# A mixture-of-experts feed-forward's scratch rows renumbered by chunk, its results stored two tiles at a time

## Chip, cores and metric

One core of one Trainium2 chip runs the whole program. The metric is the device time in microseconds, lower is better. The engines are TensorE (PE, its weight loads PEld), VectorE (DVE), ScalarE (ACT), GpSimd (POOL) and SyncE (SP), which here only issues transfers.

## The reference, cut to what matters

Two layers act on x, [4, 512, 256] float32, that is 16 tiles of 128 tokens. Layer 0 is cross attention and a small mixture of experts; layer 1 is cross attention with 16 heads and then this feed-forward, which the change touches:

```
def _L1_ffn_ref(x, router_w, router_b, w1, b1, w2, b2, sw1, sb1, sw2, sb2):   # E = 64, K = 8, H = 64
    xf = x.reshape(-1, d_)
    probs = jax.nn.softmax(xf @ router_w + router_b, axis=-1)
    tw, ti = jax.lax.top_k(probs, K)
    tw = tw / jnp.sum(tw, axis=-1, keepdims=True)
    ...  # routed: sum over the 64 experts of cw[:, None] * (silu(xf @ W1 + B1) @ W2 + B2)
    return (routed + shared).reshape(b_, s_, d_)   # shared: two dense experts of width 512
x = x + _L1_ffn_ref(_layernorm(x, axis=-1), ...)
```

## The kernel before, in words

Everything is written out by hand: each engine has one program (`d_sync`, `d_pe`, `d_act`, `d_dve`, `d_pool` for the last feed-forward), and semaphores join them. `wait_from(engine, semaphore, value)` is such a wait.

**The routed experts.** The 64 experts form 32 pairs of 64 + 64 hidden columns. The tokens are taken in two halves g = 0, 1 of 8 tiles. Each of the 8 x 1024 (token, expert) choices of a half gets a position: positions are grouped by pair and each pair starts on a multiple of 128, so the half has NX = 95 tiles of 128 rows, of 256 floats (1 KB) each. `x_starts`, `x_positions` and `x_places` work the positions out on DVE: `x_rk` holds the position of each token at each expert, `dve.max` (L2185) takes the eight of a token, and L2187 converts them to integers, `x_at`. POOL reads `x_at` in `x_scatter` (L2289), which writes the normalised token rows into the HBM scratch `zs2[g]` by 64 indirect transfers of 128 rows, and later in `x_gather` (L2325), which reads the result rows from `ys2[g]` by 64 more. `x_sum` (L2336) adds them, weighted, to X on DVE. `zs2` is first filled with zeros (`x_fill`, L1976). Layer 0's small expert stage works in the same way on scratch of its own, and loads its chunks into `e_z`.

**The loop over tiles.** The 2 x 95 = 190 tiles (GXN) run through one loop of all engines. A chunk is four tiles of a half (the last has three), 24 chunks a half. SP loads a chunk with one transfer (`load_chunk`, L2404) into one of three buffers `xt_z`: a partition gets four rows of 1 KB which lie 128 rows apart in HBM. PE transposes tile q + 3 (L2461), ACT copies it to `xt_zt` (L2553, four buffers) and copies the pair's weights to `xt_w1c` (L2569), PE multiplies tile q + 2 (L2471), ACT applies silu (L2579), DVE masks (L2650), PE multiplies tile q by the second weights (L2492), and DVE copies the result from PSUM to `xt_y` (L2658, four buffers of one tile). SP stores each tile by a transfer of its own, 128 rows of 1 KB (L2416).

**The order on SP's queue** is written out: in `d_sync`, L2411 to L2416, for every tile q: if q begins chunk c, first issue the load of chunk c + 2; then wait for `y_out` of tile q and issue its store. So the load of chunk c + 2 is issued behind the store of the last tile of chunk c - 1. The load of the second half's first chunk also waits for the second scatter (L2401).

**Where the plan is made.** The first half's planning runs on DVE between pieces of attention (`routing` in `w_dve`, x_places at unit 24), the second half's inside the loop (`tick` of `d_dve`: ranks at q = 2, places at q = 3, owners at q = 10, tables at q = 14). DVE does the ticks in order between its masks and copies, and from q = 110 on eight sums (L2343) in every ten ticks. Behind the loop, `d_dve` splits the second shared expert's weights and runs the shared experts of u = 2 to 7 (`d_hidden`, `second`); the second half's gather and sums run beside them, and the program ends with the last 32 sums and the store of X.

Of the kernel before, what the change touches and what calls it, by code (L numbers as in the profile page):

```python
# [5 lines left out]
F32 = mybir.dt.float32  # L6
# [9 lines left out]
P = 128  # L16
# [23 lines left out]
NYX = 4  # L40
# [36 lines left out]
def build_program(nc, x, ctxT, ctx, mask, cols, rows, l0_wqT, l0_wkT, l0_wv, l0_w1, l0_w2, gate_wT,  # L77
                  mlp1, mlp2, mlp1_bT, mlp2_b, l1_wp, router_w, l1_w1, l1_w2, l1_b2,
                  x1_w1, x1_w2, x1_b1, out):
    with ExitStack() as ctx_all:  # L80
# [56 lines left out]
        zs2 = [nc.dram_tensor(f"zs2{g}", [NX * P, D], F32).ap() for g in range(2)]  # L137
        ys2 = [nc.dram_tensor(f"ys2{g}", [NX * P, D], F32).ap() for g in range(2)]
# [148 lines left out]
        xt_y = [sb(f"xt_y{i}", [P, D]) for i in range(NYX)]  # L287
# [3 lines left out]
        xt_zt = [sb(f"xt_zt{i}", [P, KD, P]) for i in range(4)]  # L291
# [4 lines left out]
        xt_s = [sb(f"xt_s{i}", [P, P]) for i in range(3)]  # L296
        x_k.append([sb(f"x_k{j}1", [P, XT_N, TOP1])[:, :, :] for j in range(3)])
# [1656 lines left out]
        PL_N, OWN_N = 11, 11  # L1954
# [21 lines left out]
        def x_fill(sp, g, part):  # L1976

            if g == 0 and part == 0:
                wait_from(sp, XR["zero"], 1)
            n0, n1 = part * 12, min(part * 12 + 12, NX)  # L1980
            sp.dma_start(zs2[g][n0 * P:n1 * P].rearrange("(n p) d -> p n d", p=P),
                         x_zero[:, :].unsqueeze(1).to_broadcast([P, n1 - n0, D])).then_inc(XR[f"fill{g}"][0], 16)
        FILLS = -(-NX // 12)
# [197 lines left out]
        def x_places(dve, g):  # L2181

            wait_from(dve, XR["pos"], 2 * g + 2)
            for i in range(XT_N):
                dve.max(x_top[g][:, i, :], x_rk[:, i, :]).then_inc(XR["top"][0], 1)  # L2185
            wait_from(dve, XR["top"], (g + 1) * XT_N)
            dve.tensor_copy(x_at[g], x_top[g]).then_inc(XR["at"][0], 1)  # L2187
# [121 lines left out]
        def x_stored(eng, q):  # L2309
            for i in range(NYX):  # L2310
                wait_from(eng, XT[f"stored{i}"], 16 * len(range(i, q, NYX)))

# [12 lines left out]
        def x_gather(pool, g):  # L2325
            x_stored(pool, (g + 1) * NX)
# [49 lines left out]

        def chunk_at(q):
            g, n = q // NX, q % NX
            return g * NXC + n // 4, n % 4
# [6 lines left out]
        def d_sync(sp):  # L2386
# [8 lines left out]
            def load_chunk(c):  # L2395
                g, qs = c // NXC, chunk_tiles(c)
                if c % NXC == 0:
                    x_all_scattered(sp, g)
                if c < 3:
                    sp.wait_ge(DM["y"], 1)  # L2400
                else:  # L2401
                    wait_from(sp, XT["t"], chunk_tiles(c - 3)[-1] + 1)
                n0 = qs[0] % NX
                sp.dma_start(xt_z[c % 3][:, 0:len(qs), :],  # L2404
                             zs2[g][n0 * P:(n0 + len(qs)) * P].rearrange("(n p) d -> p n d", p=P)).then_inc(XT[f"zin{c % 3}"][0], 16)
# [5 lines left out]
            for q in range(GXN):  # L2411
# [3 lines left out]
                wait_from(sp, XT["y_out"], q + 1)  # L2415
                sp.dma_start(ys2[q // NX][q % NX * P:(q % NX + 1) * P], xt_y[q % NYX][:, :]).then_inc(XT[f"stored{q % NYX}"][0], 16)  # L2416
# [3 lines left out]
        def d_pe(pe):  # L2420
# [43 lines left out]
            def first(q):  # L2464
# [5 lines left out]
                for k in range(KD):  # L2470
                    last = pe.matmul(PS[:, 2 + q % 2, 0:P], xt_w1c[q % 3][:, k, :], xt_zt[q % 4][:, k, :], start=k == 0,  # L2471
                                     stop=k == KD - 1)
# [65 lines left out]
        def d_act(act):  # L2538
# [10 lines left out]
            def turned(q):  # L2549
# [3 lines left out]
                act.activation(xt_zt[q % 4][:, :, :], PS[:, q % 2, 0:D].rearrange("p (k t) -> p k t", k=KD), ACT.Copy  # L2553
# [66 lines left out]
        def d_dve(dve):  # L2620
# [32 lines left out]
            def out_of(q):  # L2653
# [59 lines left out]
            split(1)  # L2713
            for u in range(FIRST, DU):
# [1182 lines left out]
```

## Time and profile before

| | |
|---|---|
| median of 3 runs | 1397.46 us (1397.35 to 1398.76) |
| the profiled execution's own time | 1403.52 us |
| its span in the trace | 1401.3 us |
| mean granted TensorE clock | 0.974 |
| busy: PE / PEld / DVE / ACT / POOL | 92% / 71% / 70% / 63% / 31% |
| the loop over the 190 tiles | about 1033 to 1302 us |
| transfers: `ys<-xt_y` / `xt_z<-zs` | 190 of 128 KB / 46 of 512 KB and 2 of 384 KB |

Times are microseconds from the span's start. An engine's idle time is put down to what released it. In a row of the timeline, the bracket at the end holds the idle time before the work and its releaser. SPq rows are the issues of transfers on SP's queue; the transfer itself lasts beyond its issue. The DMA share is the mean busy share of the core's 16 DMA engines.

### The profile page before, as it was taken

The page shows a single profiled execution, that of the slowest core. Times are in us where ns is not written, and L with a number is a line of the kernel's source. Part 1 is how long each engine was busy: PE and PEld are TensorE (multiplying, and loading weights), DVE is VectorE, ACT ScalarE, POOL GpSimd, SP SyncE. Part 2 cuts the span into 40 slices and gives each one's busy share as a digit, 9 for nine tenths or more (in the row PEclk, how much of TensorE's full clock was granted, in tenths as well). Part 3 has the DMA queues.
Part 4 walks back from the last instruction along what each step waited for, and adds up shares of the span by engine and source line. Part 5 has one row for each costly group of instructions (what it writes and reads, how often), then busy time and mean ns, then how long its engine had stood idle before and what let it go on. Part 6 is the DMA issues. An engine that isn't in the chain of part 4 may idle for free.

```text
span 1401.3 us, 28443 instructions
## 1 busy us (share of the span) xinstructions
PE 1290.4 (92%) x9262; PEld 997.0 (71%) x9262; DVE 983.5 (70%) x2775; ACT 879.2 (63%) x2147; POOL 436.3 (31%) x457
## 2 busy tenths in 40 slices
PE   7999998997999979999999999999978999988993
PEld 6899897885556656667676666666676777777893
DVE  7767764465656768887788887988547655777665
ACT  5556664334766656777787785778436777777540
POOL 0000001234055160610001000677206763454574
PEclk9999999999999999999999999999989999999997
DMA  9522200413365230332632400232356887888343
GB/s 349 201 77 74 76 24 17 164 76 121 132 194 192 75 95 3 111 102 99 202 126 87 159 17 9 76 122 84 133 201 225 298 290 231 255 268 259 102 133 98
DMA packets 147627, 194.65 MB, mean 139 GB/s; under 512 B 14639, under 2 KB 129941, under 8 KB 146453
## 3 DMA queue, kind: packets, MB, share of 16 engines
q1 hardware_dynamic: 132117, 150.79, 32.3%
q0 software_dynamic: 15360, 41.96, 9.3%
q8 instruction: 81, 1.33, 0.4%
q14 instruction: 69, 0.57, 0.1%
HBM read 107.77 MB, written 84.93 MB: 138 GB/s over the span
## 4 chain that ended last, share of the span: by engine, by line
PE 66%; DVE 14%; DMA 7%; ACT 5%; issue 5%; POOL 1%; ACTq 1%; SPq 0%; DVEq 0%; POOLq 0%
PE PS L72 9%; PE PS L73 8%; PE PS L74 8%; PE PS L3292 7%; DMA xt_z<-zs 6%; PE PS L1416 6%; PE PS L3264 5%; PE PS L2471 3%; PE PS L3279 3%; PE PS L2492 3%; PE PS L3307 3%; PE PS L1432 2%; DVE a_pt L971 2%; PE PS L1310 2%; PE PS L2461 2%
## 5 line engine op out<-in xcount | busy, mean ns | idle before, releaser
L3414 ACT ACTIVATE c_pt<-PS 100x512 f32<-100x512 f32 x256 | 138.8, 595 | 92.3 <-PE PS L3279 91.7
L3405 ACT ACTIVATE c_pr<-c_sm,c_mn 128x400 f32<-128x400 f32 x256 | 158.8, 626 | 18.1 <-DVE c_mn L3554 18.1
L3554 DVE CUSTOM_DVE_ANT_0 c_sm<-PS,c_mw 128x400 f32<-128x400 f32 x256 | 136.0, 568 | 11.1 <-PE PS L3264 9.7
L2471 PE MATMUL PS<-xt_zt,xt_w1c 128*128 128x128 f32 x760 | 124.0, 287 | 9.2 <-ACT xt_w1c L2569 5.5
L3292 PE MATMUL PS<-c_pt,c_v 100*64 100x512 f32 x512 | 125.8, 613 | 0.0
L3264 PEld LDWEIGHTS PS<-c_k,c_q 64*128 64x128 f32 x768 | 63.0, 189 | 82.9 <-issue 49.8
L2492 PE MATMUL PS<-xt_w,xt_h 128*128 x380 | 116.2, 388 | 3.7 <-DVE xt_y L2658 3.6
L2471 PEld LDWEIGHTS PS<-xt_zt,xt_w1c 128*128 128x128 f32 x760 | 102.7, 197 | 20.8 <-ACT xt_w1c L2569 19.2
L3264 PE MATMUL PS<-c_k,c_q 64*128 64x400 f32 x768 | 106.3, 382 | 9.2 <-DVE c_mn L3554 8.6
L449 POOL TENSOR_TENSOR rs<-ve,halfneg 128x4 f32<-128x4 f32 x12 | 13.8, 1147 | 321.0 <-DVE ve L464 228.3
L3563 DVE TENSOR_SCALAR c_pr<-c_pr,c_rl 128x400 f32<-128x400 f32 x256 | 106.8, 459 | 4.5
L2553 ACT ACTIVATE xt_zt<-PS 128x256 f32<-128x256 f32 x190 | 72.2, 381 | 57.1 <-PE PS L2461 56.4
L1416 PE MATMUL PS<-e_w,e_zt 128*128 x184 | 90.9, 618 | 3.3 <-issue 1.6
L2461 PE MATMUL PS<-ident,xt_z 128*128 128x128 f32 x380 | 75.6, 282 | 16.8 <-DMA xt_z<-zs 12.8
L2658 DVE COPY xt_y<-PS 128x256 f32<-128x256 f32 x190 | 79.7, 419 | 15.8 <-DMA ys<-xt_y 14.2
L2569 ACT ACTIVATE xt_w1c<-xt_w 128x256 f32 x190 | 78.1, 412 | 18.8 <-issue 18.6
L2332 POOL DMA_INDIRECT xt_rows<-ys,R x64 | 62.5, 977 | 75.3 <-DVE X L2343 30.0
L2461 PEld LDWEIGHTS PS<-ident,xt_z 128*128 128x128 f32 x380 | 51.7, 143 | 43.7 <-DMA xt_z<-zs 23.7
L3279 PEld LDWEIGHTS PS<-ident,c_pr 64*100 64x100 f32 x2048 | 76.7, 126 | 8.5 <-issue 0.8
L3279 PE MATMUL PS<-ident,c_pr 64*100 64x64 f32 x2048 | 79.3, 218 | 0.0
L2332 POOL DMA_INDIRECT xt_rows<-ys,x_keep x64 | 63.9, 998 | 36.8 <-issue 18.9
L2300 POOL DMA_INDIRECT zs<-x_stage,R x64 | 64.9, 1014 | 19.3 <-issue 17.1
(407 smaller groups left out, 3488.2 us busy)
## 6 DMA issues: line engine op xcount, KB each, us to landing
ys<-xt_y SPq DMA_DIRECT2D x190, 128.0 KB
xt_z<-zs SPq DMA_DIRECT2D x46, 512.0 KB
zs<-x_zero SPq DMA_DIRECT2D x14, 1536.0 KB, 6.9
xt_w<-x_w SPq DMA_DIRECT2D x4, 2048.0 KB, 15.3
a_cT<-ctxT SPq DMA_DIRECT2D x4, 1601.0 KB
a_raw_nat<-ctx SPq DMA_DIRECT2D x4, 1536.0 KB
zs<-e_zero SPq DMA_DIRECT2D x2, 2944.0 KB, 19.4
ys<-e_y SPq DMA_DIRECT2D x46, 128.0 KB
```

The costliest lines, as they stand in the source:

```text
L72: pe.matmul(out, w[0], x[0], start=first, stop=False)
L1416: last = pe.matmul(PS[:, 2 + q % 2, :], e_zt[q % 3][:, k, :], w[:, 0, k, :], start=False, stop=k == KD - 1, skip_group_check=True)
L2332: pool.indirect_dma_start(x_rows(n)[:, k, :], None, ys2[g][:, :], bass.IndirectOffsetOnAxis(ap=x_at[g][:, i, k:k + 1], axis=0)).then_inc(x ...
L2461: last = pe.transpose(PS[:, q % 2, k * P:(k + 1) * P], xt_z[c % 3][:, n, k * P:(k + 1) * P], ident[:, :])
L2471: last = pe.matmul(PS[:, 2 + q % 2, 0:P], xt_w1c[q % 3][:, k, :], xt_zt[q % 4][:, k, :], start=k == 0, stop=k == KD - 1)
L2492: pe.matmul(PS[:, 4 + q % 2, 0:D], xt_h[q % 3][:, :], xt_w2[:, bass.ds(pair[q], 1), :].squeeze(1), start=True, stop=True).then_inc(XT["y"] ...
L3264: last = pe.matmul(PS[:, BS + h, 0:WIN], c_q[u % 2][a][hs, i * P:(i + 1) * P], c_k[u % 2][c][hs, :], start=n == 0, stop=n == 2)
L3279: last = pe.transpose(PS[0:KW, BT + r, (h * 4 + t) * DH:(h * 4 + t + 1) * DH], c_pr[s % 3][h][half, t * KW:(t + 1) * KW], ident[half, half])
L3292: last = pe.matmul(PS[h * DH:(h + 1) * DH, BU, :], c_v[ph % 2][0:KW, t, p * P + h * DH:p * P + (h + 1) * DH], c_pt[u % 2][0:KW, h, t, :], ...
L3405: act.activation(c_pr[s % 3][h][:, :], c_sm[h][:, :], ACT.Exp, bias=c_mn[:, s % 4, h:h + 1], scale=-1.0, accum_out=c_l[:, s % 4, h:h + 1]) ...
L3414: act.activation(c_pt[u % 2][0:KW, :, :, i * P + r * DH:i * P + (r + 1) * DH].rearrange("p h t q -> p (h t) q"), PS[0:KW, BT + r, :].rearr ...
L3554: dve.tensor_tensor_reduce(c_sm[h][:, :], PS[:, BS + h, 0:WIN], c_mw[:, b * QT + i, :], 1.0, BIG, ALU.add, ALU.min, c_mn[:, s % 4, h:h + 1 ...
```

## The change

Rows of `zs2` and `ys2` are renumbered. Before, row p of tile n of a half was row 128 n + p. After, in chunk c = n // 4, it is row 512 c + 4 p + n % 4, so that the four rows of a partition lie together. `x_places` works the new number out of the old one by nine more operations of DVE on [128, 64] floats, in seven steps that wait for each other, ahead of the conversion; it borrows three slices of `x_rk` as scratch. A load of a chunk then takes 4 KB per partition from one place. The result tiles are stored by two: `xt_y` has three buffers of two tiles, and SP issues one transfer of 2 KB per partition when the second tile is done (48 a half; the last of a half carries one tile). `xt_y` moves in SBUF to beside `xt_z`, where it overlaps `d_h`, so DVE waits for all stores (`x_stored(dve, 1)`) before the shared experts; `xt_zt` has three buffers for four. The scratch tensors grow from 95 to 96 tiles, and the fill with them.

```diff
-        zs2 = [nc.dram_tensor(f"zs2{g}", [NX * P, D], F32).ap() for g in range(2)]
+        zs2 = [nc.dram_tensor(f"zs2{g}", [4 * NXC * P, D], F32).ap() for g in range(2)]
...
-        xt_y = [sb(f"xt_y{i}", [P, D]) for i in range(NYX)]
...
-        xt_zt = [sb(f"xt_zt{i}", [P, KD, P]) for i in range(4)]
+        xt_zt = [sb(f"xt_zt{i}", [P, KD, P]) for i in range(2)]
+        xt_y = [sb(f"xt_y{i}", [P, 2, D]) for i in range(NYX)]
...
+        xt_zt.append(sb("xt_zt2", [P, KD, P]))
...
             for i in range(XT_N):
                 dve.max(x_top[g][:, i, :], x_rk[:, i, :]).then_inc(XR["top"][0], 1)
-            wait_from(dve, XR["top"], (g + 1) * XT_N)
-            dve.tensor_copy(x_at[g], x_top[g]).then_inc(XR["at"][0], 1)
+            top = g * TOP_N + XT_N
+            tile, chunk, at = (x_rk[:, h, :].rearrange("p (i k) -> p i k", k=TOP1) for h in range(3))
+            wait_from(dve, XR["top"], top)
+            dve.tensor_scalar(tile, x_top[g], 0.5 - P / 2, 1.0 / P, ALU.add, ALU.mult).then_inc(XR["top"][0], 1)
+            dve.tensor_scalar(at, x_top[g], 4.0, None, ALU.mult).then_inc(XR["top"][0], 1)
+            wait_from(dve, XR["top"], top + 2)
+            dve.tensor_scalar(chunk, tile, 1.5 * BIG23, None, ALU.add).then_inc(XR["top"][0], 1)
+            wait_from(dve, XR["top"], top + 3)
+            dve.tensor_scalar(tile, chunk, 1.5 * BIG23, None, ALU.subtract).then_inc(XR["top"][0], 1)
+            wait_from(dve, XR["top"], top + 4)
+            dve.tensor_scalar(chunk, tile, -1.5, 0.25, ALU.add, ALU.mult).then_inc(XR["top"][0], 1)
+            dve.scalar_tensor_tensor(at, tile, 1.0 - 4 * P, at, ALU.mult, ALU.add).then_inc(XR["top"][0], 1)
...
+            dve.scalar_tensor_tensor(tile, chunk, 4.0 * (P - 1), at, ALU.mult, ALU.add).then_inc(XR["top"][0], 1)
+            wait_from(dve, XR["top"], top + 9)
+            dve.tensor_copy(x_at[g], tile).then_inc(XR["at"][0], 1)
...
+        def in_chunk(rows, c):
+            at = c % NXC * 4 * P
+            return rows[c // NXC][at:at + 4 * P].rearrange("(p n) d -> p n d", n=4)
+
+        def two_at(q):
+
+            n = q % NX
+            return q // NX * NX2 + n // 2, n % 2, n % 2 == 1 or n == NX - 1
...
-                n0 = qs[0] % NX
-                sp.dma_start(xt_z[c % 3][:, 0:len(qs), :],
-                             zs2[g][n0 * P:(n0 + len(qs)) * P].rearrange("(n p) d -> p n d", p=P)).then_inc(XT[f"zin{c % 3}"][0], 16)
+                sp.dma_start(xt_z[c % 3][:, 0:len(qs), :], in_chunk(zs2, c)[:, 0:len(qs), :]).then_inc(XT[f"zin{c % 3}"][0], 16)
...
-                wait_from(sp, XT["y_out"], q + 1)
-                sp.dma_start(ys2[q // NX][q % NX * P:(q % NX + 1) * P], xt_y[q % NYX][:, :]).then_inc(XT[f"stored{q % NYX}"][0], 16)
+                j, m, last = two_at(q)
+                if last:
+                    wait_from(sp, XT["y_out"], q + 1)
+                    sp.dma_start(in_chunk(ys2, c)[:, n - m:n - m + 2, :], xt_y[j % NYX][:, :, :]
+                                 ).then_inc(XT[f"stored{j % NYX}"][0], 16)
...
-                wait_from(dve, XT[f"stored{q % NYX}"], 16 * (q // NYX))
-                dve.tensor_copy(xt_y[q % NYX][:, :], PS[:, 4 + q % 2, 0:D]).then_inc(XT["y_out"][0], 1)
+                j, m, last = two_at(q)
+                if m == 0:
+                    wait_from(dve, XT[f"stored{j % NYX}"], 16 * (j // NYX))
+                dve.tensor_copy(xt_y[j % NYX][:, m, :], PS[:, 4 + q % 2, 0:D]).then_inc(XT["y_out"][0], 1)
...
             split(1)
+            x_stored(dve, 1)
```

## Rows read from the trace of the kernel before

**Rows 1.** The page: the span; the chain that ended last by line.

```profile
span 1401.3 us, 28443 instructions
...
PE PS L72 9%; PE PS L73 8%; PE PS L74 8%; PE PS L3292 7%; DMA xt_z<-zs 6%; PE PS L1416 6%; PE PS L3264 5%; PE PS L2471 3%; PE PS L3279 3%; PE PS L2492 3%; PE PS L3307 3%; PE PS L1432 2%; DVE a_pt L971 2%; PE PS L1310 2%; PE PS L2461 2%
```


**Rows 2.** Window, L2461 alone: PE, PEld (counts), clock, DMA share, GB/s.

```profile
1084.20:1285.80 201.60, 59.51 (x302) 40.60 (x302) 0.99 0.85 268
```


**Rows 3.** Timeline: first matmuls of two chunks that waited for no load.

```profile
1244.24 0.71 PE L2471 MATMUL PS<-xt_zt,xt_w1c 128*128 128x128 f32 x4
...
1249.01 0.71 PE L2471 MATMUL PS<-xt_zt,xt_w1c 128*128 128x128 f32 x4
```


**Rows 4.** Chain of waits in order of time (start us, us, what): two loads.

```profile
1180.48 6.70 DMA xt_z<-zs
...
1236.18 6.37 DMA xt_z<-zs
```


**Rows 5.** Waits, 1040 to 1304 us: us in total, times, longest.

```profile
PEld PS L2461 <- DMA xt_z<-zs: 23.7, 30, 2.5
...
DVE xt_y L2658 <- DMA ys<-xt_y: 14.2, 18, 2.0
```


**Rows 6.** Timeline: a load's issue, and the transpose that needed it.

```profile
1252.47 0.47 SPq L2404 DMA_DIRECT2D xt_z<-zs  x1
...
1257.49 0.44 PE L2461 MATMUL PS<-ident,xt_z 128*128 128x128 f32 x2 [0.33 <-DMA xt_z<-zs]
```


**Rows 7.** Tile xt_z: issues of its loads (ns min/median/max).

```profile
L2404 SPq DMA_DIRECT2D xt_z<-zs x48: 371/434/2008, 1018.3 to 1291.4; - x48
```


**Rows 8.** Windows: PE, PEld, DVE, ACT, POOL busy; PEclk, DMA share, GB/s.

```profile
1016.00:1020.00 4.00, 2.99 (x27) 2.68 (x25) 1.57 (x4) 1.34 (x2) 0.00 (x0) 1.00 0.99 426
1123.00:1143.00 20.00, 18.51 (x125) 15.10 (x124) 10.59 (x30) 14.67 (x47) 16.00 (x16) 1.00 0.89 297
1163.00:1183.00 20.00, 18.83 (x127) 15.37 (x126) 10.79 (x33) 15.05 (x47) 4.28 (x5) 1.00 0.69 212
1187.00:1192.00 5.00, 4.78 (x23) 4.14 (x24) 1.89 (x5) 2.71 (x8) 3.78 (x5) 0.66 1.02 363
```


**Rows 9.** The tile x_stage: POOL's second scatter, first and last start.

```profile
L2300 POOL DMA_INDIRECT zs<-x_stage,x_keep x64: 957/971/1117, 1058.1 to 1148.6; - x64
```


**Rows 10.** DMA issues by line: KB each, median us from issue to landing.

```profile
e_z<-zs SPq DMA_DIRECT2D x9, 512.0 KB, 4.3
...
out<-X SPq DMA_DIRECT2D x4, 512.0 KB, 3.4
```


**Rows 11.** Timeline of DVE: small dependent operations; the conversion.

```profile
870.64 0.18 DVE L2157 TENSOR_SCALAR x_cq<-x_cp 128x32 f32<-128x32 f32 x1
870.86 0.18 DVE L2159 TENSOR_SCALAR x_cp<-x_cq 128x32 f32<-128x32 f32 x1
...
881.64 0.20 DVE L2187 CAST R<-R 128x64 int32<-128x64 f32 x1
```


**Rows 12.** Timeline of PEld: the next scores wait for DVE.

```profile
884.82 0.48 PEld L3264 LDWEIGHTS PS<-c_k,c_q 64*128 64x128 f32 x6 [0.81 <-DVE c_mn L3554]
```


**Rows 13.** Timeline: the second half's conversion, then PE.

```profile
1056.27 0.20 DVE L2187 CAST x_keep<-x_keep 128x64 int32<-128x64 f32 x1
...
1057.39 0.69 PE L2492 MATMUL PS<-xt_w,xt_h 128*128 x2 [1.91 <-DVE xt_y L2658]
```


**Rows 14.** Timeline of POOL: the first issue of each gather.

```profile
1177.50 1.02 POOL L2332 DMA_INDIRECT xt_rows<-ys,R  x1 [27.93 <-DMA ys<-xt_y]
...
1305.03 1.90 POOL L2332 DMA_INDIRECT xt_rows<-ys,x_keep  x1 [17.57 <-DMA ys<-xt_y]
```


**Rows 15.** Timeline behind the loop: DVE's split, last sums, last gather.

```profile
1304.88 1.23 DVE L2642 TENSOR_TENSOR d_w<-d_w1r,d_w 128x1024 fp32r<-128x1024 f32 x1
...
1384.58 13.27 DVE L2343 SCALAR_TENSOR_TENSOR X<-xt_rows,x_keep,X 128x256 f32<-128x256 f32 x25
...
1386.93 1.14 POOL L2332 DMA_INDIRECT xt_rows<-ys,x_keep  x1 [0.30 <-issue]
```

More of the change, by code:

```diff
@@ L39 @@
 NXC = -(-NX // 4)
-NYX = 4
+NX2 = -(-NX // 2)
+NYX = 3
 HEADS, DH = 16, 64
@@ L136, in build_program @@
         ys = [nc.dram_tensor(f"ys{g}", [NB * P, D], F32).ap() for g in range(GR)]
-        zs2 = [nc.dram_tensor(f"zs2{g}", [NX * P, D], F32).ap() for g in range(2)]
-        ys2 = [nc.dram_tensor(f"ys2{g}", [NX * P, D], F32).ap() for g in range(2)]
+        zs2 = [nc.dram_tensor(f"zs2{g}", [4 * NXC * P, D], F32).ap() for g in range(2)]
+        ys2 = [nc.dram_tensor(f"ys2{g}", [4 * NXC * P, D], F32).ap() for g in range(2)]
         def col(name, j):
@@ L1953, in build_program @@
         PIECES = 7
-        PL_N, OWN_N = 11, 11
+        PL_N, OWN_N, TOP_N = 11, 11, XT_N + 9
         FIELD = (NP - 1).bit_length()
@@ L1979, in x_fill @@
                 wait_from(sp, XR["zero"], 1)
-            n0, n1 = part * 12, min(part * 12 + 12, NX)
+            n0, n1 = part * 12, min(part * 12 + 12, 4 * NXC)
             sp.dma_start(zs2[g][n0 * P:n1 * P].rearrange("(n p) d -> p n d", p=P),
                          x_zero[:, :].unsqueeze(1).to_broadcast([P, n1 - n0, D])).then_inc(XR[f"fill{g}"][0], 16)
-        FILLS = -(-NX // 12)
+        FILLS = -(-4 * NXC // 12)
         def x_router_sync(sp):
@@ L2185, in x_places @@
                 dve.max(x_top[g][:, i, :], x_rk[:, i, :]).then_inc(XR["top"][0], 1)
-            wait_from(dve, XR["top"], (g + 1) * XT_N)
-            dve.tensor_copy(x_at[g], x_top[g]).then_inc(XR["at"][0], 1)
+            top = g * TOP_N + XT_N
[10 more added lines that the diff above has]
+            dve.scalar_tensor_tensor(at, tile, 1.0 - 4 * P, at, ALU.mult, ALU.add).then_inc(XR["top"][0], 1)
+            wait_from(dve, XR["top"], top + 6)
+            dve.tensor_scalar(tile, chunk, 1.5 * BIG23, None, ALU.add).then_inc(XR["top"][0], 1)
+            wait_from(dve, XR["top"], top + 7)
+            dve.tensor_scalar(chunk, tile, 1.5 * BIG23, None, ALU.subtract).then_inc(XR["top"][0], 1)
+            wait_from(dve, XR["top"], top + 8)
+            dve.scalar_tensor_tensor(tile, chunk, 4.0 * (P - 1), at, ALU.mult, ALU.add).then_inc(XR["top"][0], 1)
+            wait_from(dve, XR["top"], top + 9)
+            dve.tensor_copy(x_at[g], tile).then_inc(XR["at"][0], 1)
         def x_owners(dve, g):
@@ L2307, in x_all_scattered, with x_stored @@
                 wait_from(eng, XR[f"scat{g}{i}"], XT_N // 2 * TOP1 * 16)
-        def x_stored(eng, q):
+        def x_stored(eng, g):
             for i in range(NYX):
-                wait_from(eng, XT[f"stored{i}"], 16 * len(range(i, q, NYX)))
+                wait_from(eng, XT[f"stored{i}"], 16 * len(range(i, (g + 1) * NX2, NYX)))
         def x_rows(n):
@@ L2325, in x_gather @@
         def x_gather(pool, g):
-            x_stored(pool, (g + 1) * NX)
+            x_stored(pool, g)
             for i in range(XT_N):
@@ L2470, in first @@
                 for k in range(KD):
-                    last = pe.matmul(PS[:, 2 + q % 2, 0:P], xt_w1c[q % 3][:, k, :], xt_zt[q % 4][:, k, :], start=k == 0,
+                    last = pe.matmul(PS[:, 2 + q % 2, 0:P], xt_w1c[q % 3][:, k, :], xt_zt[q % 3][:, k, :], start=k == 0,
                                      stop=k == KD - 1)
@@ L2552, in turned @@
                     act.wait_ge(DM["y"], 1)
-                act.activation(xt_zt[q % 4][:, :, :], PS[:, q % 2, 0:D].rearrange("p (k t) -> p k t", k=KD), ACT.Copy
+                act.activation(xt_zt[q % 3][:, :, :], PS[:, q % 2, 0:D].rearrange("p (k t) -> p k t", k=KD), ACT.Copy
                                ).then_inc(XT["zt"][0], 1)
```

## The prediction

> **What bounds the kernel now.** I read the page first: its chain is mostly matmuls, but one transfer stands among them, `xt_z<-zs`, with 6% of a span of 1401.3 us, about 80 us in a stage that has only 190 tiles [rows 1]. That share overstates what can be won, since PE works during most of a load. So I measured the loop against itself. The window over the transposes counts 302 matmuls of L2461 in 201.6 us, two a tile, so 151 tiles at 1.335 us [rows 2]. Where no load is late, the first matmuls of two neighbouring chunks lie 1249.01 - 1244.24 = 4.77 us apart, 1.193 us a tile [rows 3]. 151 tiles at that pace are 180.1 us, so 21.5 us of the stretch are lost. The chain of waits in order of time shows where: it passes through 14 loads, up to 6.37 and 6.70 us from issue to the transpose [rows 4]. The waits of the loop agree in size: PEld waited 30 times, 23.7 us, for a load; DVE waited 18 times, 14.2 us, for a store that still held its `xt_y` [rows 5].
>
> Why are the loads late? One is issued at 1252.47, and the transpose that needs it starts at 1257.49 after an idle time of 0.33: at the unstalled pace a load has some 4.7 us from issue to need [rows 6]. The issue of a load has a median of 434 ns but a longest of 2008 ns: SP's queue is then held up itself [rows 7]. And the DMA engines are near full: with POOL's scatter running, their share is 0.89 at 297 GB/s, against 0.69 at 212 where POOL is mostly idle [rows 8]. POOL's 64 scatters start over 90.5 us, one of 128 KB each 1.44 us [rows 9]; the loop at its unstalled pace wants 2 x 128 KB each 1.193 us beside them, together 311 GB/s, a share of 0.93 on the mean of the engines. So loads come late by what queues up.
>
> **The change, part by part.**
>
> *Cheaper packets.* From the same windows, time per KB on one of 16 engines is share x 16 x 1024 / rate: 0.89 gives 49 ns where nearly everything is 1 KB rows, 0.99 and 426 GB/s give 38 ns where the weight tables come in rows of 16 KB [rows 8]. No row shows 4 KB or 2 KB packets alone, so these two are the bounds: a gain of nothing, and of 11 ns per KB. I take a fixed part per packet plus a part per KB that fits both, 11.7 + 37.3 ns: 40.2 ns per KB for a load in 4 KB packets, 43.1 for a store in 2 KB packets. A tile needs 8 KB of each per engine and 6.6 KB of POOL's. Before that is 22.6 x 49 = 1107 ns of 1193, 93%; after it is 8 x 40.2 + 8 x 43.1 + 6.6 x 49 = 990 ns, 83%. What the engines move at the share of 0.89 rises from 297 to about 332 GB/s against 311 wanted, so the backlog should mostly go, though not all: the lead of 4.7 us stays as written, a load of 512 KB in 1 KB rows took 4.3 us even in the lightly loaded first expert stage (`e_z`), and a store of that size 3.4 [rows 10]. Its own transfer becomes 0.28 us shorter, but a store of two tiles stands in front of it instead of one, 0.3 us longer. The gain is in the queue, not in the single load.
>
> Of the 21.5 us, some 1.7 belong to the clock: behind the load of 6.70 us that landed at 1187.2 the mean granted clock was 0.66 for 5 us, a part of it at 1.2 instead of 2.4 GHz, and 5 x 0.34 = 1.7 [rows 4, 8]. The other 19.8 are load waits. Bounds: none or all of them go. I take three quarters, 14.9 us, since the computed capacity is above what is wanted but the lead is no longer, and 1 us of the clock's.
>
> The Trainium skill speaks against it ("DMA: Bandwidth & Descriptors", section "Why small descriptors are slow (HBM only)"): the cost is about 3 cycles per packet beside one per 32 bytes, and merging pays only at 256 bytes or less. By that, 1 KB costs 35 cycles and 4 KB 131, only 6% less per KB where my fit has 18%; the sum would then end near the second rival's below.
>
> *Stores by two.* 96 issues for 190, each of 0.3 us; SP mostly waits, so I count nothing. The buffers hold six tiles instead of four, and a pair is waited for five tiles behind its issue instead of nearly four: DVE's 14.2 us should nearly vanish, but they lie inside the same stalls and are not counted again.
>
> *The new row numbers.* Nine operations in seven dependent steps on DVE, twice. Small dependent operations start 0.22 us apart, and one on 128x64 lasts 0.20 against 0.18 [rows 11]. Seven steps at 0.24, two of them with a second operation at 0.1, make 1.9 us. In the first half they stand behind L2187 at 881.64, and from there to the next scores DVE is busy throughout: PE's weight load at 884.82 had waited 0.81 for DVE [rows 12]. So they are on the path: +1.9. In the second half they stand behind 1056.27, and at 1057.39 PE had waited 1.91 for DVE: again on the path, +1.9 [rows 13]. Bounds for each: nothing if later slack takes it back, 2.5 with a lower clock behind the longer wait. POOL's scatters start 1.9 us later: the second runs from 1058.1 to 1148.6, would end near 1151, and its first reader, load 24, is issued near q = 88. With the loop at full pace that is about 1159, so the wait for it stays covered by some 6 us; if that cover went, SP's queue would stand, stores included [rows 9].
>
> *The gathers* wait for the stores of their half, at 1177.50 and 1305.03. They move with the loop [rows 14]. A last store of 256 KB lands perhaps 0.4 us later, and the last gather, issued at 1386.93, serves the last 8 of the 25 sums that begin at 1384.58 and take 0.53 each, so at 1393.6, over 6 us behind its issue: covered. The new wait of DVE for all stores stands behind its split, which starts at 1304.88, about when the gather found them stored: covered too, and queued behind it is only `low` of u = 2, which waits for ACT anyway [rows 15].
>
> *Three buffers `xt_zt` for four:* PE transposes tile q + 3 only after it has multiplied tile q + 1, so no new wait. The larger fill, 256 KB more, lies in attention: nothing.
>
> **Sum.** 1.9 + 1.9 - 14.9 - 1.0 = -12.1 us. The profiled execution took 1403.52 (span 1401.3 and 2.2 around it), which becomes 1391.4; it lies 6.1 above the median of the runs, and against the median of 1397.46 the forecast is 1385.4. Its own range, with 60% to 90% of the load waits gone and 2 to 5 us of DVE, is 1381 to 1390.
>
> **Rivals.**
>
> *All of it goes.* No load is late: -19.8 - 1.7 + 3.8 = -17.7, so 1379.8, and down to 1377 if DVE's work is partly covered. For it: the capacity estimate, and the queue's held issue of 2 us. Against it: the lone 4.3 us of `e_z` are near the lead of 4.7 with nothing queued. Chance 0.15.
>
> *The packets are not cheaper.* The 38 ns may be due to the tables' stage having reads only, without stores beside them. Then 1 KB costs the same in any packet, demand stays at 93%, and only fewer issues and the deeper store buffers help: a third of the waits, -6.6 + 3.8 = -2.8, so 1394.7. Chance 0.17. The rule of the Trainium skill cited above points to this rival.
>
> *Slower: the doubled store in front of each load.* SP's queue issues a 256 KB store immediately before every load (L2404 behind L2416). If the packets are no faster, each load lands 8 x 49 = 0.39 us later. Paid at the 14 to 30 loads that are waited for, that is 5 to 12 us; with DVE's 3.8 it makes 1406 to 1413, taken as 1408. It decides if a load's own gain stays under 0.39 us and the backlog does not shrink. Against it: SP's queue carries the same bytes in a quarter of the packets. Chance 0.10.
>
> *The change does not do what it says:* the transfers are still cut into 1 KB packets, and only DVE's 3.8 us stay, 1401.3. Against it: both sides are contiguous for 4 KB and 2 KB. Chance 0.03. The forecast keeps 0.55.
>
> **How the numbers follow.** A difference under 0.2%, 2.8 us, can't be told from none. Faster: 0.55 + 0.15 and half of the second rival, 0.78; within 0.2%: its other half, 0.09; slower: the last two, 0.13. Leaving out the slow cases and half of the lowest, the range is 1377 to 1395.
>
> **What would show it.** The DMA packets should fall by some 18,200 (46 x 384 + 2 x 256) for the loads and 12,000 (94 x 128) for the stores, the DMA share in the loop to 0.8 with the rate up to 300 GB/s, and L2461's waits for a load from 23.7 to about 6 us. The 151 tiles should take some 186 us. L2187 should come 1.9 us after the last maximum in both halves. The forecast is wrong if loads still take 5 us or more while POOL runs, if load 24 waits for the scatter, or if the clock falls again behind PE's longer wait near 1058.

## The result, and the profile after

The changed kernel took 1405.27 us in the median of 20 runs (1400.04 to 1414.82), the kernel before, run beside it, 1400.03 (1395.11 to 1407.60). The ratio is 1.0035 with a 95% interval of 1.0018 to 1.0052: 5 us slower, where 12 us faster were forecast. Single runs of one kernel spread over 12 to 15 us, more than the effect; the two profiled executions have spans of 1401.3 and 1400.9 us, so their spans say nothing, and their rows must be read for what waits for what.

The page of the changed kernel, its span and its DMA packets:

```profile
span 1400.9 us, 28274 instructions
...
DMA packets 116169, 195.15 MB, mean 139 GB/s; under 512 B 13135, under 2 KB 80053, under 8 KB 114997
```

The packets fell from 147,627 to 116,169, by 31,458 where some 30,200 were forecast. So the transfers are cut as the change says. Yet the waits that this was to remove stand where they were. The loads in its chain of waits, in order of time (19 are in that chain now, 14 before) [rows 4]; PEld's wait for a load, in the waits of 1040 to 1304 us [rows 5]; and the issues of the loads, with the time from issue to landing below (min/median/max, us) [rows 7]:

```profile
1180.83 5.76 DMA xt_z<-zs
...
1240.64 6.42 DMA xt_z<-zs
```

```profile
PEld PS L2491 <- DMA xt_z<-zs: 23.6, 26, 2.2
```

```profile
L2432 SPq DMA_DIRECT2D xt_z<-zs x48: 320/432/1565, 1018.0 to 1289.6; - x48
...
DMA to landing us min/median/max: 3.5/5.1/10.1
```

23.6 us in 26 waits, where it was 23.7 in 30. A load of 4 KB rows lands after 5.1 us in the median (the trace records the landing of 16 of the 48 loads), and the lead, the time from a load's issue to the transpose that needs it, is still about 4.7.

The landing is not the same everywhere. Here are the landings and PEld's waits for a load in three stretches: beside POOL's second scatter (1058 to 1148 us), with POOL nearly idle (1150 to 1177), and beside its gathers (1180 to 1295):

```profile
DMA to landing us min/median/max: 4.5/5.0/5.3
PEld PS L2491 <- DMA xt_z<-zs: 6.1, 9, 0.9
...
DMA to landing us min/median/max: 3.7/3.9/4.2
PEld PS L2491 <- DMA xt_z<-zs: 1.5, 2, 0.8
...
DMA to landing us min/median/max: 4.8/5.6/5.8
PEld PS L2491 <- DMA xt_z<-zs: 16.0, 15, 2.2
```

So with POOL nearly idle a load lands well within its lead, beside the scatter it takes a little more than the lead, and beside the gathers, where two thirds of the waits lie, 0.9 us more. (The two waits of the middle stretch include that for a load issued at 1147.07, still beside the scatter.) DVE's 14.2 us of waiting for a store are gone; no such row is left. The window over the transposes [rows 2] holds 306 matmuls, 153 tiles, in the time in which there were 151:

```profile
1084.20:1285.80 201.60, 59.50 (x306) 40.92 (x305) 1.00 0.82 271
```

That is 2.6 us for the loop's steady part, in one execution of each kernel. The windows [rows 8], with PE, PEld, DVE, ACT, POOL busy, the granted clock, the DMA share and GB/s:

```profile
1123.00:1143.00 20.00, 18.58 (x127) 15.84 (x128) 11.21 (x32) 15.23 (x48) 16.01 (x16) 1.00 0.82 292
1163.00:1183.00 20.00, 19.24 (x131) 16.14 (x130) 11.03 (x33) 16.04 (x50) 3.45 (x4) 1.00 0.69 220
1187.00:1192.00 5.00, 4.51 (x31) 3.57 (x29) 2.31 (x7) 3.86 (x12) 3.78 (x5) 1.00 0.92 292
```

With the scatter running, the share fell from 0.89 to 0.82 at nearly the same rate (292 GB/s for 297), so packets did become cheaper there (46 ns per KB for 49); with POOL nearly idle it is 0.69 at 220 GB/s for 212. The engines have more room and the loop does not use it.

The nine new operations, from the timeline: the last maxima, the first and the conversion, and then PE behind its wait for DVE [rows 13]. In the first half, PEld behind DVE [rows 12]:

```profile
1053.80 1.12 DVE L2187 MAX8 x_keep<-x_rk 128x8 f32<-128x64 f32 x8
...
1054.95 0.20 DVE L2191 TENSOR_SCALAR x_rk<-x_keep 128x64 f32<-128x64 f32 x1
...
1056.82 0.20 DVE L2207 CAST x_keep<-x_rk 128x64 int32<-128x64 f32 x1
...
1057.97 1.21 PE L2522 MATMUL PS<-xt_w,xt_h 128*128 x2 [2.38 <-DVE xt_y L2690]
```

```profile
885.01 0.48 PEld L3297 LDWEIGHTS PS<-c_k,c_q 64*128 64x128 f32 x6 [2.10 <-DVE c_mn L3587]
```

They run from 1054.95 to 1056.82, 1.87 us, and PE's wait is 2.38 us where it was 1.91. In attention, PEld waits 2.10 us where it waited 0.81. So the waits for a load that the change was to remove are still there, and what it added stands on the path. Behind the loop, DVE's split and the gather's first issue lie as before [rows 14, 15]:

```profile
1304.41 1.23 DVE L2672 TENSOR_TENSOR d_w<-d_w1r,d_w 128x1024 fp32r<-128x1024 f32 x1
...
1305.05 1.42 POOL L2352 DMA_INDIRECT xt_rows<-ys,x_keep  x1 [19.45 <-DMA ys<-xt_y]
```

### The profile page after: what moved, and what is told of

It reads as the page before. It is cut to its first block, busy times and chain, and to the rows that moved or that the text cites. A ratio compares the mean times of both kernels' runs of the same rounds, so it can differ in the third digit from the quotient of the medians.

```text
span 1400.9 us, 28274 instructions
## 1 busy us (share of the span) xinstructions
PE 1287.7 (92%) x9262; PEld 993.0 (71%) x9262; DVE 986.2 (70%) x2793; ACT 879.9 (63%) x2147; POOL 438.5 (31%) x457
## 2 busy tenths in 40 slices
DMA packets 116169, 195.15 MB, mean 139 GB/s; under 512 B 13135, under 2 KB 80053, under 8 KB 114997
## 4 chain that ended last, share of the span: by engine, by line
PE 64%; DVE 15%; DMA 8%; ACT 5%; issue 5%; POOL 1%; ACTq 1%; SPq 0%; DVEq 0%; POOLq 0%
PE PS L73 9%; PE PS L74 8%; PE PS L75 8%; DMA xt_z<-zs 7%; PE PS L3325 6%; PE PS L1418 6%; PE PS L3297 5%; PE PS L3312 3%; PE PS L2501 3%; PE PS L3340 3%; PE PS L1434 2%; PE PS L2522 2%; DVE a_pt L973 2%; PE PS L1312 2%; DVE c_sm L3587 2%
## 5 line engine op out<-in xcount | busy, mean ns | idle before, releaser
L2599 ACT ACTIVATE xt_w1c<-xt_w 128x256 f32 x190 | 78.1, 412 | 18.5 <-issue 18.3
L2491 PEld LDWEIGHTS PS<-ident,xt_z 128*128 128x128 f32 x380 | 52.3, 144 | 44.3 <-DMA xt_z<-zs 23.6
## 6 DMA issues: line engine op xcount, KB each, us to landing
xt_w<-x_w SPq DMA_DIRECT2D x4, 2048.0 KB, 14.9
```

What stands on the lines that cost most here:

```text
L2491: last = pe.transpose(PS[:, q % 2, k * P:(k + 1) * P], xt_z[c % 3][:, n, k * P:(k + 1) * P], ident[:, :])
```

## The experiments

Two theories stood against each other. **L**: a load is late because its own time from issue to landing is longer than its lead on SP's queue. **Q**: it is late because the DMA engines lack capacity and a backlog builds up. Each ratio is against the kernel before, timed beside it, with its 95% interval.

### The plan operations alone, and the change without them

```diff
 # e1, on the kernel before: the new operations, their result not used
+            top = g * TOP_N + XT_N
+            tile, chunk, at = (x_rk[:, h, :].rearrange("p (i k) -> p i k", k=TOP1) for h in range(3))
...
+            wait_from(dve, XR["top"], top + 9)
             dve.tensor_copy(x_at[g], x_top[g]).then_inc(XR["at"][0], 1)
```

> Edit: the kernel before, with the nine new operations of DVE in x_places, whose result is not used (old row numbers, old loads and stores). Theory L (a load is late by its own time from issue to landing, against a lead of some 4.7 us, and not by a backlog of the DMA engines; the change then leaves the load waits as they are and costs only DVE's planning): +2 to +4 us over before, 1.001 to 1.003, most of the change's loss; the second half's conversion comes 1.87 us later and the rest of the loop is as before. Rival S (the loss comes from the stores by two that stand in front of the loads): about +1 us or none, since there is neither a longer store nor another load here.

```diff
 # e2, on the changed kernel: the nine operations out, everything else in
-            dve.tensor_scalar(tile, x_top[g], 0.5 - P / 2, 1.0 / P, ALU.add, ALU.mult).then_inc(XR["top"][0], 1)
...
-            dve.tensor_copy(x_at[g], tile).then_inc(XR["at"][0], 1)
+            dve.tensor_copy(x_at[g], x_top[g]).then_inc(XR["at"][0], 1)
```

> Edit: the changed kernel with the nine operations left out, so that rows are scattered and gathered by the old numbers while loads and stores use the new layout (tiles then hold rows of other pairs; the amount and order of work is the same). Theory L: within 2 us of before (0.999 to 1.001), with load waits of PEld in the loop still 20 to 25 us. Rival S: still +3 us or more. A third theory, Q (packets did ease the DMA engines and DVE's planning ate the gain): 3 us or more faster than before, with load waits under 18 us.

e1 took 1406.64 us against 1399.92, ratio 1.0039 (1.0023 to 1.0056). e2 took 1398.23, ratio 0.9978 (0.9957 to 0.9998). The operations alone cost 5.5 us (0.0039 of 1399.9; 3.2 to 7.8), as much as the whole change loses and more than the 2 to 4 expected; the layout and the stores by two gain 3 us (0.3 to 6.0). That is between what L and Q expected of e2 (under 2, over 3), but its waits are not under 18 us, as Q has it. They stand at 27.6, in an execution that was the longest of the twelve (1407.87 us). And e1, whose loads have 1 KB rows, shows what the page of before did not, how long those take to land:

```profile
PEld PS L2473 <- DMA xt_z<-zs: 27.6, 27, 3.1
```

```profile
L2422 SPq DMA_DIRECT2D xt_z<-zs x48: 370/435/1976, 1018.6 to 1290.7; - x48
...
DMA to landing us min/median/max: 3.8/5.1/11.7
```

5.1 us in the median (of 32 recorded loads), the same as 4 KB rows. In the three stretches above the medians of e1 are 4.7, 4.2 and 5.6 us, those of the changed kernel 5.0, 3.9 and 5.6. So where loads are late, beside POOL's transfers, larger packets do not make them land sooner. With POOL nearly idle they may by 0.3 us, which is what the prediction computed for the load's own transfer, but that rests on four and two loads.

e1's windows show where the operations cost. Here are, in order, the kernel before from 860 to 900 us, and e1 there and from 1050 to 1070 us:

```profile
860.00:900.00 40.00, 37.15 (x310) 25.28 (x306) 33.82 (x124) 23.71 (x61) 14.38 (x14) 0.91 0.13 44
```

```profile
860.00:900.00 40.00, 35.62 (x302) 24.70 (x298) 33.61 (x127) 22.10 (x56) 12.92 (x13) 0.91 0.10 35
1050.00:1070.00 20.00, 15.14 (x86) 12.97 (x86) 14.35 (x60) 9.80 (x30) 8.96 (x9) 0.83 0.47 150
```

In attention PE is busy 1.5 us less of the same 40 (35.62 for 37.15). In the loop the mean granted clock from 1050 to 1070 is 0.83, where the kernel before has 0.91; the changed kernel has 0.81 there. PE waits longer for DVE and more of the following stretch is at 1.2 instead of 2.4 GHz, by 20 x 0.08 = 1.6 us. It was so in all four profiles that have the nine operations in one block in the loop (the changed kernel, e1 and, below, e3 and e9: 0.81 to 0.83), and in none of the ten that have none there (0.91 to 1.00). With the operations in three pieces (e10 and e14 below) it is 0.79 and 1.00. This stretch alone does not show a net price: over 1000 to 1300 us the mean granted clock is 0.97 in the kernel before, in the changed kernel and in e1 alike.

The clocks of whole executions do. Their mean is 0.9769 over the 78 runs of the kernel before that were timed beside the experiments, and 0.9745 over the 20 runs of the changed kernel, 0.9747 over 12 of e1 and 0.9750 over 6 of e3; without the nine operations it is 0.9765 (e2) and 0.9770 (e7). Among the runs of the kernel before, the 17 at 0.975 took 1403.3 us on average and the 11 at 0.980 took 1398.2, about 1 us for each 0.001. By that, e1's 0.0022 (give or take 0.0015) are worth some 2 us of its 5.5, an estimate.

### The loads issued earlier

```diff
 # e3 on the changed kernel, e4 on the kernel before
-                if n == 0 and c >= 1 and c + 2 < 2 * NXC:
-                    load_chunk(c + 2)
+                if n == 1 and c + 3 < 2 * NXC:
+                    load_chunk(c + 3)
```

> Edit: the changed kernel with each load issued three tiles earlier on SP's queue (chunk c + 3 at the second tile of chunk c, instead of chunk c + 2 at the first tile of chunk c; the buffer is free by then). Theory L: the lead grows by 3 x 1.2 = 3.6 us to about 8, over the median landing of 5.1, so PEld's waits for a load fall from 23.6 us to under 4 and the time falls by 16 to 22 us, to 0.985 to 0.990 of before. Theory Q (the DMA engines lack capacity): the waits hardly shrink, since the same bytes must pass in the same time: under 6 us gained.

> Edit: the kernel before with the same earlier loads (chunk c + 3 at the second tile of chunk c). Theory L: as in the changed kernel, load waits under 5 us and 17 to 24 us faster than before, 0.983 to 0.988, thus faster than the changed kernel with early loads by DVE's 2 to 4 us; stores of one tile may still hold DVE a little. Theory Q: less than 6 us gained, and clearly less than the changed kernel gains from the same edit, since here packets are of 1 KB.

e3 took 1383.90 us, ratio 0.9879 (0.9857 to 0.9901), e4 1392.62, 0.9936 (0.9913 to 0.9958). In neither is a wait for a load left in the loop. This is against Q: e3 passes the same bytes in 17 us less, and the landing is no shorter (5.4 us in e3). It does not tell what a landing of 5 us is made of, since the longer lead, some 8 us, covers it in any case. And e4 gained half of what L expected. Its waits, with e3's first, show what came next:

```profile
DVE xt_y L2690 <- DMA ys<-xt_y: 2.2, 6, 0.9
```

```profile
DVE xt_y L2658 <- DMA ys<-xt_y: 14.5, 24, 1.8
...
PE PS L2492 <- DVE xt_y L2658: 8.9, 12, 1.9
```

The store buffers. With a buffer of four tiles, DVE waits for stores and PE for DVE.

### Packets or store buffers

```diff
 # e5: old numbers, 1 KB rows, one store a tile, six result tiles, three xt_zt; loads three tiles earlier as above
-        xt_y = [sb(f"xt_y{i}", [P, D]) for i in range(NYX)]
+        xt_y = [sb(f"xt_y{i}", [P, 2, D]) for i in range(NYX)]       # NYX = 3, beside xt_z as in the change
...
-                sp.dma_start(ys2[q // NX][q % NX * P:(q % NX + 1) * P], xt_y[q % NYX][:, :]).then_inc(XT[f"stored{q % NYX}"][0], 16)
+                sp.dma_start(ys2[q // NX][q % NX * P:(q % NX + 1) * P], xt_y[j % NYX][:, m, :]).then_inc(XT[f"stored{j % NYX}"][0], 16)
...
-                wait_from(dve, XT[f"stored{q % NYX}"], 16 * (q // NYX))
+                if m == 0:
+                    wait_from(dve, XT[f"stored{j % NYX}"], stored_of(j % NYX, j))
 # e6: the same with the loads where they were
 # e7: the changed kernel, nine operations out, loads three tiles earlier
```

> Edit: old row numbers, no plan operations, 1 KB rows in every transfer and one store a tile, but loads issued three tiles earlier and room for six result tiles instead of four. It tells whether the gain of early loads with the new layout over the same with the old one (1383.9 against 1392.6) came from larger packets or from the deeper store buffers. Theory B (the buffers: DVE no longer waits for stores, 14.5 us in 24 waits of the kernel before with early loads): at least as fast as the changed kernel with early loads and by the plan operations' 5 us faster, 1376 to 1381, 0.983 to 0.986 of before. Theory K (the packets): 1388 to 1393, as the kernel before with early loads, since its DMA share of 0.90 stays.

> Edit: the same without the earlier loads: old numbers, 1 KB rows, one store a tile, six buffers. It is the change without its layout and without its plan operations. Theory L (loads late by their own landing time against the lead): PEld's waits for a load stay at 20 to 25 us and DVE's waits for a store vanish; 0 to 3 us faster than before, like the change without plan operations (1398.2). If the packets had a part in that, it is slower than that one by more than 2 us.

> Edit: the changed kernel without the nine operations (rows of other pairs in the tiles, the same amount of work) and with the earlier loads. Against the changed kernel with early loads it prices the nine operations again: 3 to 6 us, so 1378 to 1381. Against the old numbers with early loads and six buffers it prices the packets alone: theory B says the two agree within 2 us, theory K that this one is 8 us or more faster.

e5: 1381.40 us, 0.9859 (0.9841 to 0.9878). e6: 1403.15, 1.0004 (0.9989 to 1.0019). e7: 1379.36, 0.9844 (0.9823 to 0.9864). With early loads, six result tiles instead of four bring 11 us (e4 to e5), and the larger packets of both loads and stores 2 us more (e5 to e7), inside the intervals. e7 also prices the nine operations again, against e3: 4.9 us (0.9879 - 0.9844), to within some 4. e6 shows the other side: without the early loads, taking away DVE's waits for a store gains nothing, and the waits for a load are 30.3 us where 20 to 25 were expected (its profiled execution, too, was the longest of twelve). It is 3.6 us behind e2 (1.0004 - 0.9978). By its expectation, over 2 us meant that the packets had a part in e2's gain; the two intervals overlap, so that part is likely and not shown. PEld's wait in e6, then DVE's in e5:

```profile
PEld PS L2477 <- DMA xt_z<-zs: 30.3, 26, 3.9
```

```profile
DVE xt_y L2676 <- DMA ys<-xt_y: 5.4, 10, 1.4
```

In e6 DVE's waits for a store are gone; in e5 they are down to 5.4 us from e4's 14.5. Two waits stood in parallel, and only with both shortened does the time fall by 20 us. e5 and e7 in the stretch of the gathers, 1190 to 1280 us:

```profile
1190.00:1280.00 90.00, 86.93 (x591) 74.50 (x591) 72.86 (x208) 71.57 (x224) 49.85 (x51) 1.00 0.91 287
```

```profile
1190.00:1280.00 90.00, 87.72 (x597) 74.98 (x596) 75.12 (x214) 71.17 (x222) 49.26 (x50) 1.00 0.85 286
```

And e5 in the stretch of the second scatter:

```profile
1058.00:1148.00 90.00, 86.45 (x580) 74.06 (x579) 59.55 (x193) 69.04 (x214) 70.83 (x69) 0.98 0.92 297
```

In the gathers' stretch there is nearly equal work at equal rates (287 and 286 GB/s), the DMA share 0.91 with 1 KB rows and 0.85 with the larger. That is 0.91 x 16 x 1024 / 287 = 52 ns per KB against 49. The packets are cheaper by 6% over all traffic, and at a share of 0.91 the loop of e5 still runs nearly at full pace: PE is busy 86.93 of the 90 us.

### Half the bytes of a load

```diff
 # e8, on e2
-                sp.dma_start(xt_z[c % 3][:, 0:len(qs), :], in_chunk(zs2, c)[:, 0:len(qs), :]).then_inc(XT[f"zin{c % 3}"][0], 16)
+                sp.dma_start(xt_z[c % 3][:, 0:2, :], in_chunk(zs2, c)[:, 0:2, :]).then_inc(XT[f"zin{c % 3}"][0], 16)
```

> Edit: the changed kernel without the nine operations, and each load brings only two of the four rows of a partition, 256 KB for 512 (the other two tiles of a chunk keep old data, the work is the same). It tells how a load's 5.1 us from issue to landing divide into a part that does not depend on its bytes and its own transfer. Theory L with the time on the bytes (own transfer some 1.3 us, and 0.7 less queue behind it): median landing 4.0 to 4.4, under the lead, PEld's waits for a load under 8 us and 12 us or more faster than before. If the landing is nearly all fixed: 4.7 us or more, and waits of 15 us or more stay.

1383.60 us, 0.9890 (0.9870 to 0.9910). The landing of 256 KB in e8, of 512 KB in e7 (median us), and e8's waits:

```profile
xt_z<-zs SPq DMA_DIRECT2D x48, 256.0 KB, 3.6
```

```profile
xt_z<-zs SPq DMA_DIRECT2D x46, 512.0 KB, 5.2
```

```profile
PEld PS L2473 <- DMA xt_z<-zs: 4.8, 11, 1.2
```

3.6 against 5.2: half of the bytes take 1.6 us off, where 4.0 to 4.4 were expected as the landing. But not in every stretch. The landings beside the scatter, with POOL nearly idle and beside the gathers (the windows of above), e7's and then e8's:

```profile
DMA to landing us min/median/max: 4.2/4.9/5.5
DMA to landing us min/median/max: 3.4/3.8/5.9
DMA to landing us min/median/max: 5.2/6.0/7.0
```

```profile
DMA to landing us min/median/max: 2.9/3.4/3.8
DMA to landing us min/median/max: 3.3/3.7/4.1
DMA to landing us min/median/max: 3.5/4.2/5.4
```

The halved load lands 1.5 and 1.8 us sooner beside POOL's transfers and 0.1 us sooner without them, though these last are the medians of four loads and of two. So the 1.6 us need not be the transfer of 256 KB alone: as far as these landings show, most of what the bytes cost appears where other traffic runs beside, and e8 has less traffic too. How a landing divides into a fixed part, its own transfer and what it shares with others is not shown. At 3.6 us, less than the lead, the waits fall to 4.8 us (in the fastest of its five runs), and the order of SP's queue had not been touched. So shortening the landing works as lengthening the lead does in e3.

### The lead by one tile, and the store in front

```diff
 # e12, on e6: one tile earlier
-                if n == 0 and c >= 1 and c + 2 < 2 * NXC:
-                    load_chunk(c + 2)
+                if n == len(chunk_tiles(c)) - 1 and c + 3 < 2 * NXC:
+                    load_chunk(c + 3)
 # e11, on e2: the load between the wait for the chunk's last tile and the store of its last pair
                 if last:
                     wait_from(sp, XT["y_out"], q + 1)
+                    if q + 1 < GXN and chunk_at(q + 1)[1] == 0 and c + 3 < 2 * NXC:
+                        load_chunk(c + 3)
```

> Edit: old numbers, 1 KB rows, single stores, six result buffers, and each load one tile earlier (before the wait for the last tile of the chunk in front) instead of three. With no lead added this kernel took 1403.2 with load waits of 30 us, with three tiles 1381.4 with none. Theory L: the lead is then 4.7 + 1.2 = 5.9 us, over the landings of 4.3 to 4.5 before the gathers and about the 5.6 beside them, so most of the gain is there: waits under 8 us, 1382 to 1388. If the waits were a matter of the DMA engines' load rather than of the lead, a third of the shift brings a third of the gain: about 1396.

> Edit: the changed kernel without the nine operations, with each load issued just before the pair store that stood in front of it, at the same moment otherwise. It tests the rival of the doubled store. If a store of 256 KB in front makes the load late: median landing 0.4 us or more below 5.3, PEld's waits for a load 5 us or more below 27.6 and 4 us or more faster than 1398.2. If not: landing down by under 0.2 and a time within 2 us of it.

e12: 1384.62 us, 0.9876 (0.9849 to 0.9904), with the waits for a load at 10.3 us for e6's 30.3 (under 8 were expected). One tile brings 18.5 of the 22 us that three tiles bring. e11: 1395.09, 0.9951 (0.9933 to 0.9968), 3 to 4 us under e2. Their waits, e12's first:

```profile
PEld PS L2477 <- DMA xt_z<-zs: 10.3, 12, 2.1
```

```profile
PEld PS L2473 <- DMA xt_z<-zs: 17.8, 21, 1.9
...
DVE xt_y L2672 <- DMA ys<-xt_y: 15.6, 22, 1.7
```

In e11 the waits for a load are 17.8 us for e2's 27.6, though the median landing only went from 5.3 to 5.1: a load is also issued 0.3 us sooner, before the store's own issue. DVE's waits for a store are back with 15.6 us, since the pair store now stands behind 512 KB. The 3 to 4 us are at the edge of what the intervals can tell from nothing, and the 0.3 us of lead would alone bring some of it, since 1.2 us brought 18.5 in e12. So if the doubled store in front of each load has a price, it is some 3 to 4 us with the lead's part in it, less than the 5 to 12 of the rival in the prediction; the time lies between the expectation's two cases.

### Where the plan operations cost

```diff
 # e9 and e13, on the kernel before: the nine operations under "if g == 1:" and "if g == 0:"
 # e10, on e3: in three pieces
+                if (u, i) in ((24, 1), (24, 2), (25, 0)):
+                    x_numbers(dve, 0, ((24, 1), (24, 2), (25, 0)).index((u, i)))
...
+                if 5 <= q < 8:
+                    x_numbers(dve, 1, q - 5)
 # e14: in three pieces in the loop (q = 5, 6, 7) only
```

> Edit: the kernel before with the nine operations of x_places in the second half only, where they stand in the loop (result unused). In both halves together they cost 5.5 us (1.0039). If the second half costs their own 1.9 us and a longer stretch at the lower clock behind PE's longer wait (mean granted clock from 1050 to 1070 us 0.83 with them against 0.91 without, 20 x 0.08 = 1.6 us): 3.5 us, 1.0025. If the first half, in attention, carries most: under 1.5 us here.

> Edit: the kernel before with the nine operations of x_places in the first half only, in attention (result unused). If the two halves add up to the 5.5 us of both together and the second half costs 1.7 us (1.0012): 3 to 4 us, 1.002 to 1.003. If each costs its own 1.9 us: 1.0013, and the loop starts 1.9 us later or less.

> Edit: the changed kernel with earlier loads, and its nine operations in three pieces: in the first half behind pieces 1, 2 and 4 of attention's unit 24 to 25 instead of all at the start of unit 24, in the second half at ticks 5, 6 and 7 instead of all at tick 3. If their price is that they stand in one block on DVE while PE waits for it: 2 to 4 us less than 1383.9, so 1380 to 1382, and PE's wait for DVE behind the conversion falls from 2.4 to under 2 us. If it is DVE's plain time: unchanged, 1383 to 1385.

> Edit: the changed kernel with earlier loads; its nine operations in one block in the first half as the change has them, and in three pieces at ticks 5, 6 and 7 in the second half. With the loop's 3.6 us gained and no later start: 1380 to 1382 (0.985 to 0.987), 2 to 4 us under the 1383.9 of the block in both halves, and level with old numbers, early loads and six buffers (1381.4).

e9: 1401.61 us, 1.0012 (0.9990 to 1.0034). e13: 1404.61, 1.0018 (1.0003 to 1.0034). 3.5 us were expected of e9 and 3 to 4 of e13; the ratios give 1.7 and 2.5. Together that is 0.0030 of the 0.0039 that both cost; the intervals allow equal shares. e13's window in attention shows PE's loss alone, 35.42 busy of 40 where the kernel before has 37.15. The five profiles with the block in attention have 35.4 to 35.6 there, e9 without it 37.11:

```profile
860.00:900.00 40.00, 35.42 (x302) 24.69 (x300) 33.57 (x129) 21.96 (x56) 13.70 (x13) 0.91 0.12 40
```

e10: 1387.13 us, 0.9903 (0.9875 to 0.9931), not 2 to 4 us better than e3 as expected but 3 us worse, which the intervals allow to be nothing. e14: 1379.42 us, 0.9845 (0.9821 to 0.9868). DVE's copies in the loop, their first and last start, e10 and then e14:

```profile
L2695 DVE COPY xt_y<-PS x190: 406/417/425, 1048.0 to 1284.6; 128x256 f32<-128x256 f32 x190
```

```profile
L2695 DVE COPY xt_y<-PS x190: 404/417/426, 1044.1 to 1281.5; 128x256 f32<-128x256 f32 x190
```

In e10 the loop runs from 1048.0 to 1284.6, 236.6 us where e3 needs 240.2 (1044.6 to 1284.8); but it starts 3.4 us later. Spread in the loop only, the start is 1044.1 and the end 1281.5. e10 and e14 differ in the first half alone, so spreading the operations over attention costs 8 us (0.9903 - 0.9845; some 3 to 13). I take it that the pieces hold DVE at more places at which the next scores wait: from 860 to 1045 us PEld waits 17.8 us for DVE before the scores in e10, at most 4.4 at once, and 15.4 us, at most 2.4, in e14. In the loop the spreading gains some 4.8 us (e3 to e14, 0.9879 - 0.9845; hardly clear of noise), and the mean granted clock of e14's runs is 0.9770 where e3's is 0.9750. e14 computes the reference in full and is the fastest full version, 22 us under the kernel before; e5, with the old numbers and no operation added, is within 2 us of it.

## Why the prediction was wrong

**The step that failed** is "so the backlog should mostly go", with its term "I take three quarters, 14.9 us": that capacity gained by cheaper packets turns into loads that land sooner. The capacity came in part (a share of 0.82 for 0.89 beside the scatter, 46 ns per KB for 49), but loads beside POOL's transfers landed no sooner (5.0 and 5.6 us, with 1 KB rows 4.7 and 5.6), and the load waits went from 23.7 to 23.6 us. The first of the prediction's own signs of being wrong, "if loads still take 5 us or more while POOL runs", is just that; the third, the lower clock near 1058, came too.

The size of the stalls (21.5 us in the stretch, 19.8 without the clock) was right: early loads and deeper buffers gain 20 us (e5). Their cause, "loads come late by what queues up", was half right. Traffic beside a load does lengthen it, as far as the stretches show: 3.9 us with POOL nearly idle, 5.6 beside the gathers, against a lead of 4.7. But the share of 0.93 that was worked out is no limit: beside the scatter e5 runs at 0.92 and 297 GB/s without a late load. A load of 512 KB takes 4 to 6 us by what runs beside it, whatever its rows, and was issued 4.7 us ahead. The prediction had written down both numbers: a lead of 4.7 us "as written", 4.3 us for `e_z` in a lightly loaded stage. It did not take the remaining 0.4 us as all the room there was.

**The price of packets.** Forecast 18% less per KB for loads and 12% for stores. The scatter's windows give 49 and 46 ns per KB, the gathers' 52 and 49, with POOL's 1 KB rows among them: 6% over all, where the prediction's own 1107 and 990 ns per tile are 11%. The Trainium skill ("DMA: Bandwidth & Descriptors", "Why small descriptors are slow (HBM only)") speaks of a small fixed cost per packet, worth merging only at 256 bytes or less. The traces agree in kind: little was there to win, 6% per KB and some 2 us between e5 and e7. The prediction cited it for its second rival, the packets that are not cheaper, in which a third of the waits goes by fewer issues and deeper buffers. Not even that went: 23.6 us are left of 23.7.

**The plan operations.** 1.9 us each was right as their length (1.87 measured), and that both are on the path was right. The term was 3.8 us, the cost 5.5 (3.2 to 7.8). The difference is within the interval, and it fits the some 2 us of the lower clock in the runs of e1, which the bound named and the sum left out. The halves measured 1.7 and 2.5 us, each to within 2 or 3.

**The stores by two.** Counted at nothing, with DVE's 14.2 us "inside the same stalls": right (e6, 1.0004). What the prediction missed is that they become the bound once loads are early, 11 us between e4 and e5.

**The slower rival,** a doubled store in front of each load, has at most a part in it, some 3 to 4 us (e11), and layout and stores together still gain 3 us (e2). The sum is then 5.5 - 3.1 = 2.4 us against a measured 4.9 (2.5 to 7.3), which the intervals cover. The covered terms held: load 24 was issued at 1157.3, behind the last scatter at 1150.1, and the last gather and DVE's new wait cost nothing.

Not settled: why a load beside POOL's transfers takes 1 to 2 us more than one without them although the engines' share is 0.81 to 0.84 there; no run took POOL's traffic away, and the stretches alone speak for it. Nor is it settled whether the 2 us between e5 and e7 are more than noise.

## What to carry to other kernels

When a wait for a transfer stands on the path, compare its time from issue to landing with the lead before looking at bandwidth: here 5.1 us against 4.7, and with store buffers deep enough, one line that issues the load a tile earlier was worth 18.5 us, the packing of its bytes 2 to 4, which may be noise. Compare them stretch by stretch: the landing went from 3.9 to 5.6 us with what ran beside it. A DMA share of 0.9 does not by itself make the DMA engines the bound; the test is whether the work goes faster when issued earlier. And small operations on an engine that others wait for can cost more than their length, here 5.5 us for 3.8, with a lower mean clock: put them where that engine has slack, and measure, since spreading them helped in one stage and hurt in the other.

## What the runs showed of the hardware

512 KB from HBM to 128 partitions took 5.1 us to land in rows of 1 KB and of 4 KB alike (medians of e1 and of the changed kernel): 4.2 and 3.9 us with GpSimd nearly idle, 4.7 and 5.0 beside its scatter, 5.6 and 5.6 beside its gathers. 256 KB took 3.7, 3.4 and 4.2 us there (e8). A chain of nine small operations of VectorE on [128, 64] floats took 1.87 us.

The clock: in the stretch from 1050 to 1070 us, a wait of PE for DVE of 2.4 us (the changed kernel) or 3.8 to 3.9 (e1, e3, e9) instead of 1.9 went with a mean granted clock lower by 0.08 to 0.10. Over whole executions of the kernel before, 0.001 of mean granted clock went with about 1 us of 1401: 17 runs at 0.975 took 1403.3 us on average, 11 at 0.980 took 1398.2.
